# Penalties of absent edges laid into PSUM by ScalarE in a two-layer graph transformer

## What is computed

```python
q = (x @ wq + bq).reshape(n, H, C)          # n = 3125, H = 2 heads, C = 64
k = (x @ wk + bk).reshape(n, H, C)
v = (x @ wv + bv).reshape(n, H, C)
alpha = jnp.einsum('ehc,ehc->eh', q[dst], k[src]) / jnp.sqrt(C)
amax = jax.ops.segment_max(alpha, dst, num_segments=n)
ex = jnp.exp(alpha - amax[dst])
denom = jax.ops.segment_sum(ex, dst, num_segments=n)
a = ex / (denom[dst] + 1e-16)
out = jax.ops.segment_sum(a[:, :, None] * v[src], dst, num_segments=n).mean(axis=1)
return out + x @ ws + bs
```

## Time and profile before

| what | us |
|---|---|
| median of 3 runs (3877.21 to 3879.16) | 3877.22 |
| the profiled execution | 3871.49 |
| its span, first to last instruction | 3869.6 |
| PE busy in the span | 3063.6 |
| POOL busy | 2811.3 |
| DVE busy | 2706.2 |
| ACT busy | 669.4 |

### The profile page before, as it was taken

One profiled execution on the slowest core, in us unless ns is written; L12 is line 12 of the kernel. 1 busy time (PEld: TensorE's weight loads), 2 busy tenths in 40 slices (PEclk: granted clock), 3 DMA queues, 4 the chain that ended last, 5 costly groups with the idle time before them and its releaser, 6 DMA issues.

```text
span 3869.6 us, 56741 instructions
## 1 busy us (share of the span) xinstructions
PE 3063.6 (79%) x18659; PEld 1701.0 (44%) x18659; DVE 2706.2 (70%) x8606; ACT 669.4 (17%) x868; POOL 2811.3 (73%) x1917
## 2 busy tenths in 40 slices
PE   4787778777777877787778777876788888799996
PEld 3555555555555555555555555543222222322222
DVE  4666666666666666666666666656888888678786
ACT  2000000000000000000000000014343444043343
POOL 3588888888888888888888888872576776088684
PEclk7988898889889988988898889888799999699998
DMA  8411111111111111111111111113544452223330
GB/s 310 152 13 13 12 13 13 12 13 13 13 12 13 13 13 12 13 13 13 12 13 13 13 13 13 13 7 71 162 140 128 134 145 71 58 77 87 76 77 9
DMA packets 244257, 194.37 MB, mean 50 GB/s; under 512 B 146300, under 2 KB 224981, under 8 KB 244181
## 3 DMA queue, kind: packets, MB, share of 16 engines
q1 hardware_dynamic: 86035, 159.92, 13.9%
q0 software_dynamic: 137984, 26.19, 11.9%
q10 hardware_dynamic: 20162, 7.27, 0.9%
HBM read 112.79 MB, written 80.42 MB: 50 GB/s over the span
## 4 chain that ended last, share of the span: by engine, by line
DMA 28%; PE 20%; issue 19%; POOL 19%; DVE 9%; ACT 2%; SPq 2%; POOLq 1%; DVEq 0%; ACTq 0%
DMA edge_counts<-small 27%; POOL nodes_and_gaps L397 10%; POOL edge_counts L406 8%; PE PS L1121 7%; PE PS L1144 6%; PE PS L1153 3%; DVE counts_and_logs L886 2%; DVE scores L898 2%; DVE PS L910 2%; SPq L329 2%; DVE scores L925 1%; PE PS L1101 1%; PE PS L1133 1%; DMA edge_counts<-counts_and_logs 1%; PE PS L1127 0%
## 5 line engine op out<-in xcount | busy, mean ns | idle before, releaser
L1037 PE MATMUL PS<-scores 128*128 128x320 bf16 x11760 | 1839.8, 321 | 537.5 <-DVE scores L765 537.5
L1037 PEld LDWEIGHTS PS<-scores 128*128 128x128 bf16 x11760 | 1222.7, 105 | 1166.6 <-DVE scores L765 546.7
L406 POOL DMA_INDIRECT edge_counts<-small x752 | 1208.2, 1607 | 264.8 <-issue 264.8
L397 POOL DMA_INDIRECT nodes_and_gaps<-xj_rows,small x784 | 800.1, 1021 | 289.7 <-issue 129.2
L445 POOL TENSOR_TENSOR scores<-scores,max_of_targets 125x896 f32<-125x896 f32 x320 | 730.0, 2321 | 382.4 <-ACT max_of_targets L597 382.4
L726 DVE SCALAR_TENSOR_TENSOR scores<-PS,small,scores 128x256 bf16<-128x256 f32 x784 | 332.8, 480 | 666.6 <-PE PS L1017 666.5
L765 DVE TENSOR_SCALAR scores<-scores,small 128x192 bf16<-128x192 bf16 x3920 | 745.2, 296 | 3.5
L898 DVE TENSOR_TENSOR scores<-PS,counts_and_logs 125x896 f32<-125x896 f32 x350 | 377.5, 1082 | 146.7 <-PE PS L1153 61.1
L1121 PE MATMUL PS<-q_features,k_features 64*125 64x448 f32 x1400 | 383.6, 632 | 108.5 <-DVE scores L898 104.9
L602 ACT ACTIVATE scores<-scores 125x896 f32<-125x896 f32 x350 | 328.4, 948 | 360.2 <-POOL scores L445 346.6
L1144 PE MATMUL PS<-scores,v_nodes 125*64 125x448 f32 x1400 | 352.2, 591 | 20.3 <-ACT scores L602 20.3
(11 more groups left out here) (162 smaller groups left out, 1714.9 us busy)
## 6 DMA issues: line engine op xcount, KB each, us to landing
counts_and_logs<-edge_counts SPq DMA_DIRECT2D x70, 980.0 KB
edge_counts<-counts_and_logs SPq DMA_DIRECT2D x50, 766.0 KB
edge_counts<-counts_and_logs SPq DMA_DIRECT2D x35, 980.0 KB
nodes_and_gaps<-xj_rows,small POOLq DMA_INDIRECT x784, 2.5
edge_counts<-small POOLq DMA_INDIRECT x752
counts_and_logs<-edge_counts SPq DMA_DIRECT2D x70, 113.8 KB
scores<-in_edge_attr_dram ACTq DMA_DIRECT2D x95, 48.0 KB
edge_counts<-counts_and_logs SPq DMA_DIRECT2D x35, 113.8 KB
```

What stands on the lines that cost most here:

```text
L397: pool.indirect_dma_start(gx[u][:, s * F:(s + 1) * F], None, xj_dram, bass.IndirectOffsetOnAxis(ap=dcur[u][:, s:s + 1], axis=0)).then_inc( ...
L406: pool.indirect_dma_start(cnt_dram, bass.IndirectOffsetOnAxis(ap=index[:, s:s + 1], axis=0), value[:, s:s + 1], None, compute_op=ALU.add). ...
L1037: ins = nc.tensor.matmul(PS[:, b, 0:HI * F], onehot[:, s, b * P:b * P + 128], spread[:, s, i].rearrange("p h f -> p (h f)"), start=first a ...
```

## The change

The logarithms are now taken in both layers, and nothing is steepened or stored. Instead ScalarE writes exp(-4.09 L - 97.2) into the tile's slot of PSUM, for both heads, where L is the logarithm of twice the count: close to nothing for an edge, a very large number where there is none. The matmul of q k no longer starts its sum anew but adds to what lies in the bank. The q features are made with a negative sign, so that the bank holds penalty minus q k, and VectorE takes logarithm minus bank. The wait of `scores` for `scored` (and, at tile 20, for `attended`) moves to `lay_gap` on ACT, and `scores` waits for `gap_laid`. In ACT's order the laying of tile i+3 stands behind the Exp of tile i; `next_h` is one iteration earlier; layings of tiles 0 and 1 of the next block stand between `copy_sums` and `spread`, and that of tile 2 behind `begin_max`.

```diff
-                if CBUFS <= k < CH * QUINTS + CBUFS:
-                    sp.wait_ge(sem("gaps_stored"), 32 * (k - CBUFS + 1))
                 if k >= CBUFS:
                     sp.wait_ge(sem("scored"), QN * (k - CBUFS + 1))
...
             for k in range(2 * CH * QUINTS):
                 load(k)
-                if CBUFS - 1 <= k < CH * QUINTS + CBUFS - 1:
-                    store(k - CBUFS + 1)
...
+                def lay_gap(c, i):
+
+                    n = l * ATT + c * NT + i
+                    k = n // QN
+                    act.wait_ge(sem("logged"), k + 1)
+                    if n >= 2:
+                        act.wait_ge(sem("scored"), n if i == PP else n - 2 if i == PP + 1 else n - 1)
+                    if c >= 2 and i == PP + 1:
+                        act.wait_ge(sem("attended"), l * CH + c - 1)
+                    nc.scalar.activation(score_slot[slot_of(i)], C5[k % CBUFS][:, i % QN].unsqueeze(1).to_broadcast([P, HEADS, D]), ACT.Exp,
+                                         scale=-GAP_SCALE, bias=BC[0:P, 17:18]).then_inc(sem("gap_laid"), 1)
...
                 for c in range(CH + 1):
+                    if c == 0:
+                        act.wait_ge(sem("k_copied"), CH * (l + 1))
+                        act.wait_ge(sem("q_copied"), CH * (l + 1))
+                        lay_gap(0, 0)
+                        lay_gap(0, 1)
                     if c < CH:
                         begin_max(c)
+                        lay_gap(c, 2)
                     for i in range(NT):
                         if c:
                             exps(c - 1, i)
-                        if l == 0 and c >= 2 and i == PART + 2:
+                        if l == 0 and c >= 2 and i == PART + 1:
                             next_h(c - 2)
+                        if c < CH and i + LEAD < NT:
+                            lay_gap(c, i + LEAD)
                         k = QUINTS * (l * CH + c) + i // QN + 2
-                        if c < CH and i % QN == 2 and i < NT - QN and k < CH * QUINTS:
+                        if c < CH and i % QN == 2 and i < NT - QN and k < 2 * CH * QUINTS:
                             logs(k)
                     if c:
                         copy_sums(c - 1)
+                    if c + 1 < CH:
+                        lay_gap(c + 1, 0)
+                        lay_gap(c + 1, 1)
                     if c < CH:
                         spread(c)
                     if c:
                         copy_spread(c - 1)
                     k = QUINTS * (l * CH + c) + QUINTS + 1
-                    if c < CH and k < CH * QUINTS:
+                    if c < CH and k < 2 * CH * QUINTS:
                         logs(k)
...
-                def steepen(k):
-
-                    dve.wait_ge(sem("logged"), k + 1)
-                    nc.vector.scalar_tensor_tensor(C5[k % CBUFS], C5[k % CBUFS], STEEP, C5[k % CBUFS], ALU.mult, ALU.min).then_inc(sem("steepened"), 1)
...
                 def score(c, i):
                     n = l * ATT + c * NT + i
                     k = n // QN
-                    if l == 0:
-                        dve.wait_ge(sem("steepened"), k + 1)
-                    else:
-                        dve.wait_ge(sem(f"count_loaded{k % CBUFS}"), 32 * (k // CBUFS + 1))
+                    dve.wait_ge(sem("logged"), k + 1)
                     if n >= SLOTS:
                         dve.wait_ge(sem("weighted_sums"), n - SLOTS + 1)
                     dve.wait_ge(sem("scores_in_psum"), n + 1)
-                    nc.vector.tensor_tensor(Ts[:, n % SLOTS], score_slot[slot_of(i)],
-                                            C5[k % CBUFS][:, i % QN].unsqueeze(1).to_broadcast([P, HEADS, D]), ALU.add).then_inc(sem("scored"), 1)
+                    nc.vector.tensor_tensor(Ts[:, n % SLOTS], C5[k % CBUFS][:, i % QN].unsqueeze(1).to_broadcast([P, HEADS, D]),
+                                            score_slot[slot_of(i)], ALU.subtract).then_inc(sem("scored"), 1)
...
                 def scores(c, i):
                     n = l * ATT + c * NT + i
-                    if n >= 2:
-                        pe.wait_ge(sem("scored"), n if i == PP else n - 2 if i == PP + 1 else n - 1)
-                    if c >= 2 and i == PP + 1:
-                        pe.wait_ge(sem("attended"), l * CH + c - 1)
+                    pe.wait_ge(sem("gap_laid"), n + 1)
                     for h in range(HEADS):
                         q = slice(F * h, F * h + F)
-                        ins = nc.tensor.matmul(score_slot[slot_of(i)][:, h, :], kT[q, i * P:(i + 1) * P], qT[q, c * D:(c + 1) * D], start=True, stop=True)
+                        ins = nc.tensor.matmul(score_slot[slot_of(i)][:, h, :], kT[q, i * P:(i + 1) * P], qT[q, c * D:(c + 1) * D], start=False, stop=True, skip_group_check=True)
                     ins.then_inc(sem("scores_in_psum"), 1)
```

More of the change, by code:

```diff
@@ L39 @@
 EMPTY = 2.0 ** -60
-STEEP = 6e28
+GAP_SCALE = 4.09
+GAP_BIAS = -97.2
 assert SLOTS == NT + LEAD
@@ L349, in load @@
                     sp.dma_start(C5[k % CBUFS][q], cnt_rows[q, g * QN:(g + 1) * QN, c * D:(c + 1) * D]).then_inc(sem(f"count_loaded{k % CBUFS}"), 16)
[L351 to L356, removed]
             sp.wait_ge(sem("sum_blocks"), 1)
@@ L581, in logs @@
                 nc.scalar.activation(C5[k % CBUFS], C5[k % CBUFS], ACT.Ln, scale=2.0).then_inc(sem("logged"), 1)
-            act.wait_ge(sem("sum_bias_set"), 1)
+            act.wait_ge(sem("sum_bias_set"), 2)
             for l in range(2):
@@ L588, in _ @@
                     act.wait_ge(sem("qk_in_psum"), 2 * (CH * l + c) + 2)
-                    nc.scalar.activation(qT[:, c * D:(c + 1) * D], qk_bank(2 * c + 1), ACT.Identity, scale=0.125, bias=BC[:, 12 + l:13 + l]
+                    nc.scalar.activation(qT[:, c * D:(c + 1) * D], qk_bank(2 * c + 1), ACT.Identity, scale=-0.125, bias=BC[:, 12 + l:13 + l]
                                          ).then_inc(sem("q_copied"), 1)
@@ L664, in link @@
                 dve.wait_ge(sem("vector_chain"), chain[0])
+            nc.vector.memset(BC[:, 17:18], GAP_BIAS).then_inc(sem("sum_bias_set"), 1)
             nc.vector.memset(BC[:, 18:19], 0.5e-16).then_inc(sem("sum_bias_set"), 1)
@@ L858, in _ @@
             dve.wait_ge(sem("layer_weights"), 16 * LOADS)
-            nc.vector.tensor_scalar(BC[:, 12:14], BC[:, 12:14], 0.125, None, ALU.mult).then_inc(sem("bias_scaled"), 1)
+            nc.vector.tensor_scalar(BC[:, 12:14], BC[:, 12:14], -0.125, None, ALU.mult).then_inc(sem("bias_scaled"), 1)
             link(nc.vector.memset(head_of, 0.0))
@@ L936, in outputs @@
                                             BR[0:MW, 256:320].unsqueeze(1).to_broadcast([MW, BLK, F]), ALU.add).then_inc(sem("attended"), 1)
-                if l == 0:
-                    steepen(0)
                 for c in range(CH + 1):
                     for i in range(NT):
-                        k = QUINTS * c + i // QN
-                        if l == 0 and i % QN == 0 and 0 < k < CH * QUINTS:
-                            steepen(k)
                         if c >= 2 and i in (INVERT, INVERT + 2):
```

## The result

The changed kernel takes 4003.06 us (median of four, 3995.12 to 4009.0) against 3877.22: 1.0332 times the time before, interval 1.0314 to 1.0351. The profiled execution has a span of 3998.2 us against 3869.6, 128.6 more.

A forecast was written before the change was run, and what follows sets the result against it. TensorE was taken to bound layer 1, VectorE's in-order queue layer 0. Layer 1 +76, layer 0 -9.5 and clock +14 gave +80 on 3871.5, with 5.7 to the median 3957 us; own range 3915 to 3995, 8 in 10 3880 to 4020.

The forecast's parts named there:

- The ring: Laying between VectorE's score and q k in two PSUM slots: 5.05 us a pair against 4.59, +4.9 a block.
- The logarithms: On ScalarE ahead of Exps PE waits for: 1.9 us late for i even, 0.7 for odd, 5.2 a block.
- The border: At a block's end, layings and a logarithm delay the first weights: 9.0 us for 6.83, +2.2; first border +1.3.
- next_h: One more ACT instruction ahead of a laying in layer 0: 0.5 us a block in five blocks, bounds 0 and 0.9.
- The first blocks: Each layer's block without weights: +3 us for logarithms at granted clock 0.76; layer 0's also loses 9.6 without steepening.
- The clock: TensorE's granted clock falling in the blocks: upper bound 42 us in twelve, lower 0, a third taken, +14.
- The clock rival: The clock's full bound of 42 us instead of 14, and logarithms at their full 2.07: 4022 us, chance 0.13.
- One of my signs: A granted clock under 0.9 in the blocks would show the forecast wrong and push the time over 3990.
- TensorE stays the bound: Rival: laying and logarithm covered, layer 0 falls by 88 us, 3789, with all borders 3814; faster had chance 0.20.
- The other gain: For the faster rival: POOL's subtraction gets quicker, from 2.32 us on the mean of both layers to 2.06.

The follow-up runs named there:

- no logarithms: The changed kernel without the 35 logarithms of layer 1, layings and waits kept: 3941.0 us, 1.0196 times the kernel before.
- filled border: The changed kernel with six idle matmuls of 64x448 on TensorE at each border after a block's second product: 3976.0 us, 1.0266 times the kernel before.
- moved logarithms: The changed kernel with only a block's first logarithm moved from iteration 2 to 3, or only its third from 12 to 13: 3969.7 and 3968.4 us.

## Why the prediction was right, and where it was short

The forecast was 3957 us, slower; the time is 4003. That is inside the range of 8 in 10 (3880 to 4020) and above the forecast's own range (3915 to 3995). The direction and the mechanism were right. One term was far too small, TensorE's clock.

The waits can be told from the clock by the times from one pair's sums to the next (starts of L1153, later L1151, on PE), each the value that recurs in the later blocks where the granted clock was 1.00, in layer 1 and, for the changed kernel's and the odd run's last rows, in layer 0. "Odd" is the run with the logarithms after odd tiles; (l) marks a logarithm in the pair.

| interval | before | changed | no logarithms | odd |
|---|---|---|---|---|
| 1 | 4.59 | 7.06 (l) | 5.18 | 5.18 |
| 2 | 4.59 | 5.18 | 5.18 | 5.73 (l) |
| 3 | 4.59 | 5.18 | 5.18 | 5.18 |
| 4 | 4.59 | 5.73 (l) | 5.18 | 5.73 (l) |
| 5 | 4.88 | 5.18 | 5.40 | 5.18 |
| 6 | 5.39 | 7.28 (l) | 5.39 | 5.40 |
| 7 | 4.59 | 5.18 | 5.18 | 5.72 (l) |
| 8 (tile 19) | 6.31 | 7.18 | 7.18 | 7.18 |
| 9 | 4.59 | 5.51 (l) | 5.18 | 5.51 (l) |
| 10 | 4.59 | 5.18 | 5.18 | 5.18 |
| 11 and 12 | 8.32 | 8.32 | 8.32 | 8.32 |
| 13, the border | 10.46 | 12.61 | 11.47 | 12.62 |
| sum | 67.5 | 79.6 | 74.0 | 76.9 |
| measured block of layer 1 | 68.5 | 84.4 | 75.6 | 78.9 |
| rest: the clock | 1.0 | 4.8 | 1.6 | 1.9 |

At full clock a block gains 79.6 - 67.5 = 12.1 us. The forecast for it was 72.9 / 6 = 12.15. The steps, one by one:

**The ring, right.** Forecast 5.05 us a pair, measured 5.18. Sums to score (1.08), q k (0.95) and weighted values (0.90) are exact. Score to laying took 1.18 (1.13 taken), laying to q k 1.07 (0.99 taken). Of that 0.09 is the bias operand, as the run without it shows. The kernel before had a hint of it: copying the sums with a bias (L607) and without (L608) took 633 and 535 ns for the same 448 columns, and I priced the laying by copies and Exps that have none. The ten pairs, tile 19's among them, gain 5.5 us a block where 4.9 was forecast, and not ten times 0.59: two of them took more than 4.59 before.

**The logarithms, right.** Forecast 1.9 and 0.7, measured 1.88 and 0.55 (0.33 for the last), 4.4 a block for 5.2. The run without the laying shows that they cost only in the ring, the one without layer 1's that they do cost there.

**The border, right.** At the border shown, where the granted clock was 1.00 from 3003.2 to 3012.2, they come 8.99 us after the spread (3003.19, 3012.18), against 6.83: 2.2, as forecast. So it is at two more borders of layer 0 and one of layer 1. At the other six, the first of each layer left out, it is 9.83, as q k ran at half clock.

**next_h, too low.** It stands ahead of a laying in five blocks of layer 0. In the one of them where the clock held, the pair with the last logarithm takes 6.49 and not 5.51: 1.0 for the 0.5 taken.

**The first blocks, too low.** Layer 0's runs from 2685.69 to 2742.26, 56.6 us for 59.6 before: -3.0 where -6.6 was forecast. Layer 1's runs from 3355.18 to 3412.82, 57.6 for 49.8: +7.9 where +3 was forecast. The granted clock was 0.67 in the first and 0.59 in the second, so half speed for most of the time; I had taken 0.76 from a stretch before. That the ring's loop is then longer than VectorE's pace throughout, and each logarithm falls into it, is the likely reason and not shown by a run.

**The clock, mis-sized: this step failed.** I took a third of a bound of 42 us, +14, by the argument that waits of 0.46 us resemble layer 1 and not layer 0. The argument looked at the wrong waits, and the third had no row behind it. By the table the clock takes 4.8 us of a layer 1 block where it took 1.0: 23 us in six. A layer 0 block of 86.2 is 79.6, 0.8 for next_h and 5.8 for the clock: against the same 1.0, 29 us in six. Together that is some 51 us, more than the bound. The bound was worked out for a granted clock of 0.92, which is what came (0.91 and 0.92), but from the loop of the ring alone, without the borders. Stretches at half speed lie at the long waits. Two of them, at the border of a layer 1 block and at its first logarithm:

```profile
3674.80:3677.30 2.50, 1.54 (x4) 0.50 (x4) 0.00 (x0) 2.50 (x3) 2.50 (x2) 0.50 0.00 0
3677.30:3679.80 2.50, 2.50 (x8) 0.79 (x8) 2.03 (x2) 1.89 (x3) 2.50 (x2) 0.50 0.02 7
3687.30:3689.80 2.50, 1.43 (x4) 0.26 (x4) 0.08 (x1) 2.50 (x4) 2.50 (x2) 0.73 0.88 235
3689.80:3692.30 2.50, 2.50 (x14) 0.58 (x12) 0.44 (x1) 0.29 (x1) 2.50 (x3) 0.59 0.81 213
3692.30:3694.80 2.50, 2.06 (x12) 0.49 (x8) 2.50 (x3) 1.76 (x2) 2.50 (x2) 1.00 0.00 0
```

TensorE's wait of 3.47 us at the border ends at 3675.76, in the first of these; its wait of 1.81 for the weights ends at 3688.37, in the third. The filled border and the moved logarithms show by their times that both kinds of wait have a share. The clock rival, at 4022, was nearer than the forecast. One of my signs was wrong too: I had tied a time over 3990 to a granted clock under 0.9 in the blocks, and it came with 0.91 and 0.92. The Trainium skill (TensorE: Matmul & The Clock Gate, HAM oscillation) tells of kernels whose repeated waits throttle the array again and again, and the trace of the change agrees: 0.92 for 0.98 over the same blocks.

The sum: layer 1's blocks +95.4 (forecast 72.9 and a share of the clock's 14), layer 0's +28.1 (forecast -2.9 and the other share), first blocks -3.0 and +7.9 (forecast -6.6 and +3). Together 128.4 of the span's 128.6 against 80. Of the 48 too few, 37 are the clock, 8.5 the first blocks and 2.4 next_h; pairs, logarithms and borders together came out as forecast. Part of that is luck: the pairs were 0.6 a block too low and the logarithms 0.8 too high.

**The rivals.** That TensorE stays the bound had a threshold, q k's penalty there 2.74 us after the sums, and it was not met: 3.33 in the trace (3030.22 to 3033.55). Its price was right. With the ring gone the time is 92 us under the kernel before, and I had 88. The other gain held as well: in layer 0 POOL's subtraction took 2.35 us a tile before the change,

```profile
3000.05 35.32 POOL L445 TENSOR_TENSOR scores<-scores,max_of_targets 125x896 f32<-125x896 f32 x15 [21.06 <-ACT max_of_targets L597]
```

and takes 2.05 now (30.79 for 15, from 3007.12), as layer 1 had it before. The Trainium skill (SBUF — State Buffer, Who interferes with whom) says that a VectorE instruction with two SBUF inputs contends with a GpSimd instruction that reads SBUF. The two numbers agree, since the steepening that is gone had both its inputs in SBUF. It bought nothing, as POOL was not what the blocks waited for.

## What to carry to other kernels

An engine with idle time is not free if it is put between the release of a buffer and its next use. Add up the loop of the ring with all its handoffs and compare it with the pace of the bound engine: here 5.05 to 4.59 said "slower" while the sum of work, 60 of 63 us, said "fits". An operation that was free beside the ring then costs up to its length within it, by where it stands: of 2.06 us, 1.9 after an even tile and 0.55 after an odd one. New waits of TensorE of the lengths seen here (1.8 and 3.5 us) should be priced with a lower clock behind them: it cost some 51 us here in twelve blocks. Or they should be filled.

## What the runs showed of the hardware

A bias operand from an SBUF column makes an ACT instruction 0.09 us longer: an Exp of 896 columns took 1.007 us with it and 0.917 without. At 448 columns it was 0.633 to 0.535, there between an Identity with a bias and a Copy without; an Exp of 448 columns with a bias took 0.634, so between those two the function makes no difference. And TensorE can gain from useless work: 72 matmuls of 64x448 at twelve borders, and the kernel is 26 us faster, with the granted clock at 0.95 and 0.97 for 0.91 and 0.92.
